# Recommendation model's interaction and MLP, one core: weights split on VectorE, the load order and the first chunk's gram schedule changed

## What is computed

```python
def reference(bottom_output, W0, b0, W1, b1, W2, b2, W3, b3, W4, b4):
    bottom_mlp_output = bottom_output[:, 0, :]
    interaction = jnp.einsum('bnd,bmd->bnm', bottom_output, bottom_output)
    interaction_flat = interaction[:, _TRIL_R, _TRIL_C]      # 351 pairs
    x = jnp.concatenate([bottom_mlp_output, interaction_flat, zero_pad], axis=1)
    x = jax.nn.relu(x @ W0.T + b0)      # 480 -> 1024
    x = jax.nn.relu(x @ W1.T + b1)      # 1024 -> 1024
    x = jax.nn.relu(x @ W2.T + b2)      # 1024 -> 512
    x = jax.nn.relu(x @ W3.T + b3)      # 512 -> 256
    return x @ W4.T + b4                # 256 -> 1
```

## Time and profile before

| | us |
|---|---|
| median of 3 runs | 509.24 |
| lowest and highest | 509.15, 509.42 |
| the profiled execution | 507.79 |
| its span | 506.0 |
| TensorE matmul busy | 478.7 (95%) |
| VectorE busy | 298.9 (59%) |
| ScalarE busy | 241.9 (48%) |
| GpSimd busy | 46.7 (9%) |

### The profile page before, as it was taken

The page is one execution under the profiler, slowest core; times in us unless marked ns, Lnnn a source line. Parts: engine busy times, 40 slices in busy tenths (PEclk is TensorE's granted clock), DMA queues, the critical chain, the costliest instruction groups (busy, mean ns, idle before and its releaser), DMA issues.

```text
span 506.0 us, 6672 instructions
## 1 busy us (share of the span) xinstructions
PE 478.7 (95%) x2480; PEld 401.4 (79%) x2480; DVE 298.9 (59%) x455; ACT 241.9 (48%) x579; POOL 46.7 (9%) x27
## 2 busy tenths in 40 slices
PE   5899678798999999999999999999999999999996
PEld 5899667687888888788888888788888888888874
DVE  3786999658645777858535777858535533110123
ACT  3877376465763347465553347465553411110121
POOL 0446440122230000000000000000000000000000
PEclk9999889899999999999999999999999999999998
DMA  7995055476429131446245242446223100424200
GB/s 259 375 378 191 8 166 196 154 257 241 169 96 345 66 117 61 171 168 227 83 155 189 83 110 66 153 161 229 84 84 110 58 0 1 166 95 155 83 0 2
DMA packets 17456, 72.28 MB, mean 143 GB/s; under 512 B 2448, under 2 KB 2448, under 8 KB 13328
## 3 DMA queue, kind: packets, MB, share of 16 engines
q1 hardware_dynamic: 17424, 71.86, 39.4%
HBM read 63.45 MB, written 8.40 MB: 142 GB/s over the span
## 4 chain that ended last, share of the span: by engine, by line
PE 78%; DVE 11%; issue 5%; ACT 3%; DMA 3%; SPq 0%; ACTq 0%; DVEq 0%
PE work L714 15%; PE work L715 15%; PE work L716 15%; PE gps L739 8%; PE acc L714 7%; PE acc L715 7%; PE acc L716 7%; DMA xraw<-x_t 3%; DVE turned L573 2%; ACT grams L400 1%; PE gps L726 1%; PE acc L726 1%; DVE h1l L612 1%; DVE xpad L633 1%; DVE grams L542 1%
## 5 line engine op out<-in xcount | busy, mean ns | idle before, releaser
L400 ACT ACTIVATE grams<-gps 32x216 f32<-32x216 f32 x384 | 131.5, 343 | 99.5 <-PE gps L739 95.9
L714 PE MATMUL work<-h1h,w1s 128*128 128x512 f32 x256 | 102.4, 400 | 2.0 <-DVE h1l L612 2.0
L715 PE MATMUL work<-h1h,w1s 128*128 128x512 f32 x256 | 102.0, 399 | 0.0
L716 PE MATMUL work<-h1l,w1s 128*128 128x512 f32 x256 | 101.4, 396 | 0.0
L432 ACT ACTIVATE act_out<-work,bias 128x512 f32<-128x512 f32 (+1 forms) x64 | 42.4, 663 | 101.8 <-PE work L716 99.1
L739 PEld LDWEIGHTS gps<-xs 128*128 128x128 f32 x384 | 56.9, 191 | 20.6 <-issue 7.5
L739 PE MATMUL gps<-xs 128*128 128x224 f32 x384 | 59.3, 277 | 9.9 <-DVE featL L601 5.0
L542 DVE SCALAR_TENSOR_TENSOR grams<-grams 128x216 f32<-128x216 f32 x48 | 21.5, 448 | 73.6 <-ACT grams L400 73.6
L714 PE MATMUL work<-featH,w0l 117*128 117x512 f32 (+5 forms) x160 | 58.3, 364 | 3.7 <-ACT act_out L439 3.7
L610 DVE CAST h2h<-act_out 128x512 fp32r<-128x512 f32 x40 | 17.0, 426 | 75.7 <-ACT act_out L432 75.4
L714 PEld LDWEIGHTS work<-h1h,w1s 128*128 128x128 f32 x256 | 48.5, 189 | 12.2 <-DVE h1l L612 2.1
(11 more groups left out here) (68 smaller groups left out, 579.2 us busy)
## 6 DMA issues: line engine op xcount, KB each, us to landing
xraw<-x_t SPq DMA_DIRECT2D x64, 432.0 KB, 4.8
w1s<-w_parts SPq DMA_DIRECT2D x24, 1024.0 KB, 4.8
w_parts<-w1s SPq DMA_DIRECT2D x8, 1024.0 KB, 5.6
stage<-w_t SPq DMA_DIRECT2D x8, 512.0 KB, 6.2
w0raw<-w_t SPq DMA_DIRECT2D x4, 512.0 KB, 7.2
w2raw<-w_t SPq DMA_DIRECT2D x4, 512.0 KB, 6.2
x0raw<-x_t SPq DMA_DIRECT2D x4, 256.0 KB, 5.1
w3raw<-w_t SPq DMA_DIRECT2D x1, 512.0 KB, 7.6
```

The costliest lines, as they stand in the source:

```text
L400: last = act.activation(grams2[rows, h // 2 % 2, at:at + HALF_GROUPS, :, :], src[:, :, :, q * EVEN:q * EVEN + INPUTS], ACT.Copy)
L714: pe.matmul(dst, wl, ah, start=start, stop=False)
L715: pe.matmul(dst, wh, ah, start=False, stop=False)
L716: return pe.matmul(dst, wh, al, start=False, stop=stop)
```

## The change

1. **Low parts of all weights go from GpSimd to VectorE** (`w0_lo_part`, `w1_lo_part`, `w2_lo_part`, `w3_lo_part`, and `zero_pads` for the pads of `xs`). GpSimd keeps only the identity matrix. W0's four are placed in the loop over the first chunk's slices, W1's behind layer 0 and layer 1 tiles, W2's four behind layer 1's tiles 0, 2, 4 and 6, W3's behind tile 7. The single count `w_done` becomes one for each weight.
2. **Input loads first.** Slices 0 to 3 are issued ahead of the small loads (biases, W4, b4); W0's pieces follow slices 4, 6, 7 and 9; slices (1,0) and (1,1), W1 tiles 0 and 1, slices (1,2) and (1,3), then W2 and W3.
3. **TensorE warm-up.** 13 transposes of the identity matrix are put ahead of the first gram.
4. **Two slices earlier.** `input_parts(1, 0)` and `(1, 1)` move into the loop over the first chunk's slices (its passes 13 and 14).
5. **The first chunk's gram schedule.** Halves 0 to 4 stand after steps 6, 11, 16, 21 and 26, then every three steps; a turn stands two steps ahead of its next half instead of three. Halves 4, 8, 12 and 16 are now after steps 26, 38, 52 and 64, half 31 after 113, the last turn after 119. The other chunks keep their schedule.
6. **Conversions.** W1's first two come earlier (within the left half's tiles), W2's four between the early tiles of layer 0, W3's behind W1's tile 3; W1's tiles 2 to 7 keep their places.

```diff
-        for h in range(HALVES):
-            half_at[step] = h
-            sub, behind = divmod(h - TURN_BEHIND, 2 * SLICES_SUB)
-            if behind == 0 and sub >= 0:
-                turn_at[step + APART_STEPS] = sub
-                step += TURN_STEPS
-            else:
-                step += APART_STEPS
-        turn_at[STEPS - 6] = SUBS - 1
+        def plan(starts, gap, last):
+            half_at, turn_at, step = {}, {}, None
+            for h in range(HALVES):
+                step = starts[h] if h < len(starts) else step + 3
+                sub, behind = divmod(h - 1 - TURN_BEHIND, 2 * SLICES_SUB)
+                if behind == 0 and sub >= 0:
+                    turn_at[step] = sub
+                    step += gap
+                half_at[step] = h
+            turn_at[last] = SUBS - 1
...
+        plans = [plan([6, 11, 16, 21, 26], 2, STEPS - 1)] + [plan([1], 3, STEPS - 6)] * (CHUNKS - 2) + [({}, {})]
...
-            load_x(0, 0)
-            sp.dma_start(w4raw[:, :, :], w4).then_inc(small_in, 16)
-            sp.dma_start(bias[:, :], biases).then_inc(small_in, 16)
-            sp.dma_start(bias4[:, :], b4.to_broadcast([P, 1])).then_inc(small_in, 16)
...
+            for p in range(2):
+                load_x(1, p)
+            for m in range(2):
+                load_w1(m)
+            for p in range(2, XSLOTS):
+                load_x(1, p)
+            for n in range(W2_LOADS):
+                sp.dma_start(w2_part(w2raw, n), w2[n, :, :]).then_inc(w2_in[n], 16)
+            sp.dma_start(w3raw[:, :], w3).then_inc(w3_in, 16)
             load_x0(1)
...
-            def w1_lo(m):
-                pool.wait_ge(w_hi, REST + m + 1)
-                pool.tensor_tensor(w1s[:, m % 2, 1, :], stage[:, m % 2, :], w1s[:, m % 2, 0, :].bitcast(f32),
-                                   ALU.subtract).then_inc(w_done, 1)
...
+            def w1_lo_part(m):
+                dve.wait_ge(w1_hi, m + 1)
+                dve.tensor_tensor(w1s[:, m % 2, 1, :], stage[:, m % 2, :], w1s[:, m % 2, 0, :].bitcast(f32),
+                                  ALU.subtract).then_inc(w1_done, 1)
...
+                if LEFT_AT < p < SLICES - 1:
+                    zero_pads(p - LEFT_AT - 1)
+                    input_parts(1, p - LEFT_AT - 1)
+            w1_lo_part(0)
...
+                    if c == 0 and m + 2 < MT1:
+                        w1_lo_part(m + 2)
+                    if c == 0 and m % 2 == 0:
+                        w2_lo_part(m // 2)
+                    if c == 0 and m == MT1 - 1:
+                        w3_lo_part()
...
+            for _ in range(WARM):
+                pe.transpose(acc[:, 3, 0:P], ident[:, :], ident[:, :])
```

More of the change, by code:

```diff
@@ L156, in by_sample, with w2_part @@
             return buf[:, p % XSLOTS, :].rearrange("p (b n) -> p b n", n=INPUTS)
[L158 to L163, removed]
+        def w2_part(buf, n):
+            return buf[:, n * LOAD:(n + 1) * LOAD]
         def parts(g, p):
@@ L196, in rec_program, with before @@
         STEPS = L0_STEPS + L1_STEPS + MT2 * KT2
[L197 removed]
         TURN_BEHIND = 10
[L199 to L211 removed]
+        def plan(starts, gap, last):
[8 more added lines that the diff above has]
+            turn_at[last] = SUBS - 1
+            assert sorted(turn_at.values()) == list(range(SUBS)) and max(half_at) < last < STEPS
+            return half_at, turn_at
+        plans = [plan([6, 11, 16, 21, 26], 2, STEPS - 1)] + [plan([1], 3, STEPS - 6)] * (CHUNKS - 2) + [({}, {})]
+        def before(c, step):
+            half_at, turn_at = plans[c]
             return (sum(x < step for x in half_at), sum(x < step for x in turn_at))
         LEFT, RIGHT = slice(0, CHUNK // 2), slice(CHUNK // 2, CHUNK)
[L218 to L220 removed]
+        SMALL_AFTER = 3
+        W0_AFTER = [4, 6, 7, 9]
+        W0_HI_AFTER = [3, 5, 7, 9]
+        W0_LO_AT = [5, 6, 9, 10]
+        W4_AT = 10
+        WARM = 13
         PAD_AHEAD = 2
@@ L455, in w1_hi @@
                     act.wait_ge(w1_kept[m % 2], kept(m - 2))
[L456 to L461 removed]
+                act.activation(w1s[:, m % 2, 0, :], stage[:, m % 2, :], ACT.Copy).then_inc(w1_hi, 1)
             act.wait_ge(zero_done, 2)
@@ L490, in on_tile @@
                     relu(c, layer, m, work[:, m % 2, :])
-                    if c == 0 and layer == 0 and m < EARLY + 2:
-                        w1_hi(m - EARLY)
+                    if c == 0 and layer == 0 and m == EARLY:
+                        w2_hi_part(2)
+                    if c == 0 and layer == 0 and m == EARLY + 1:
+                        w2_hi_part(3)
                 def after_tile(m):
                     if c == 0 and m + 2 < MT1:
-                        w1_hi(m + 2)
-                interleave(on_half, on_turn, on_tile, after_tile)
+                        w1_hi_part(m + 2)
+                    if c == 0 and m == 1:
+                        w3_hi_part()
+                interleave(c, on_half, on_turn, on_tile, after_tile)
                 for m in range(MT2):
@@ L660, in _ @@
                 split_left(m)
-            for p in range(AHEAD):
-                input_parts(1, p)
+            for i in range(2, XSLOTS):
+                zero_pads(i)
+            input_parts(1, 2)
             def body(c, more):
@@ L677, in on_tile @@
                             answers(c - 1)
+                        if c == 0 and m == EARLY:
+                            w1_lo_part(1)
                     else:
@@ L804, in layer2 @@
                 pe.wait_ge(split_done, nth(c, 1, k) + 1)
+                if c == 0 and k % 2 == 0:
+                    pe.wait_ge(w2_done, k // 2 + 1)
                 for m in range(MT2):
@@ L855, in after_step @@
                     if more and step in half_at:
-                        gram_half(c + 1, half_at[step], before(step)[1])
+                        gram_half(c + 1, half_at[step], before(c, step)[1])
                     if more and step in turn_at:
-                        transpose_pairs(c + 1, turn_at[step], before(step)[0])
+                        transpose_pairs(c + 1, turn_at[step], before(c, step)[0])
                     step += 1
```

118 lines of the change are left out of this document (59 added, 59 removed).

## The result

The changed kernel takes **526.67 us** (median of 4 runs, 525.4 to 527.29) beside 509.25 for the kernel before, run beside it: a ratio of 1.0331, 95% interval 1.0307 to 1.0355. It is slower by 17 us. The forecast was 523.0 with a range of 510 to 533. The profiled execution took 527.29 us, its span is 525.5, against 506.0 before.

A forecast was written before the change was run, and what follows sets the result against it. TensorE was taken to end the kernel. Layer 2 of the first chunk ends at 65.8 + 80.7 + 29 = 175.5; the next chunk starts 13.9 us later; 507.79 + 13.9 = 521.7, plus 1.45 for the median: 523 us, range 510 to 533.

The forecast's parts named there:

- steps 0 to 23 end: Rest of layer 0, right half of the columns, in the first chunk: ends at 65.8 us, 15.2 earlier.
- the four waits: First chunk after step 23: TensorE held up by late W1 loads for 3.4, 7.2, 4.7 and 7.5 us, 22.8 in all.
- half clock behind the four: After each TensorE stop for a late W1 load: matmuls at half clock cost 1.5 us.
- steps, halves, turns otherwise: First chunk after step 23, undisturbed: 96 steps, 28 gram halves and three transposes take 80.7 us.
- waits at the end: Before layer 0 of the second chunk: TensorE waits 3.9 us, 2.1 + 1.8, where it waited for nothing.
- half clock at the end: With the wait before the second chunk's layer 0: half clock costs 1.5 us more.
- the front: Start of the kernel up to the numbered steps: these begin at 53.8 us instead of 60.6.
- The wait that was off most: Second W1-load wait, first chunk: load lands at 29.1 us after step 23, TensorE stands at half 11 for 7.2 us.
- The clock term: Half clock behind TensorE's stops: 1.5 us each, bounded by zero and twice that.
- rival 3: Layer 1 tiles: VectorE becomes the bound, some 2 us more in each of six tiles, 535 us; chance 0.04.
- Rival 1: First chunk: W1 loads still land in time and TensorE runs through, 495.5 us; chance 0.12.
- Rival 2: W1-load waits are shallow: transfers land in 4.3 us and half clock fails to come, 508 us; chance 0.05.

The follow-up runs named there:

- experiment 1: Changed kernel with only SyncE's order rewritten: W1 write-backs and loads ahead of slice loads that wait for later splits; 497.43 us, ratio 0.9776 to the kernel before.
- experiment 2: Changed kernel with only the first chunk's gram schedule put back as in the kernel before; 503.06 us, ratio 0.988 to the kernel before.
- experiment 6: Changed kernel with W1's write-backs and loads of tiles 2 to 7 issued by GpSimd instead of SyncE; 497.84 us, ratio 0.9775 to the kernel before.
- experiment 5: Changed kernel with only W1 tile 0's write-back and tile 2's load moved ahead of slice (1,7) in SyncE's order; 523.64 us, ratio 1.0282.
- experiment 3: Changed kernel with an in-between gram schedule: halves 0 to 4 after steps 4, 8, 12, 16, 20, last turn after 114; 517.72 us, ratio 1.0151.
- experiment 8: experiment 1 plus eight GpSimd subtractions of 1,024 columns into a buffer nobody reads; 513.35 us, ratio 1.0089 to the kernel before.
- experiment 10: experiment 1 with halves 25 to 31 two steps apart, last turn after 117, W3's low part behind tile 5; 498.07 us, ratio 0.9776.

## Why the prediction was right, and where its sizes were off

**Direction and mechanism** are as predicted: weight loads behind slice loads whose splits the new plan puts later, ScalarE in the landing of `stage` four times, for 3.8 to 8.8 us (3 to 9 were foretold), gram copies behind it, TensorE behind those, a fifth stop before layer 0 of the second chunk. Experiments 1, 2 and 6 take the cause away in three ways and the waits go in all three.

**The sum.** Layer 0 of the second chunk starts at 185.2; predicted was 181.0. Term by term:

| | predicted | measured |
|---|---|---|
| steps 0 to 23 end | 65.8 | 66.2 |
| the four waits | 3.4, 7.2, 4.7, 7.5 = 22.8 | 3.8, 9.2, 5.5, 6.8 = 25.2 |
| half clock behind the four | 6.0 | 8.3 |
| steps, halves, turns otherwise | 80.7 | 82.4 |
| waits at the end | 3.9 | 3.1 |
| half clock at the end | 1.5, ahead of layer 0 | 1.4, behind its start |

The measured half clock is the difference of TensorE's busy time in experiment 1 (90.99 less 82.74), the row under it what is left of the 119.0 us; the last row is 342.1 us from layer 0's start to the end against 340.7 before.

The term for the undisturbed steps was 1.7 us short; TensorE's 82.74 us of busy time in experiment 1 show the same. Of that, 0.4 is a slip: with the values as printed, 96 x 0.70, 28 x 0.44 and 3 x 0.25 make 80.3 and not 80.7. Another slip is in the front: 2.1, 3.69 less 0.7 to 1, and 1.5 make 6.3 to 6.6 us and not 6.8.

**The wait that was off most** is the second. I let TensorE run on to half 11. In fact it stopped already at the turn, two steps ahead, because the turn writes to the bank that half 10's copy had not yet left; and the chain from the split of (1,7) to the landing took 8.6 us (88.69 to 97.29) where I had 7.5. **The clock term** was mis-sized too: 1.5 us for each stop came from stretches behind waits of about 3 us. Behind the wait of 9.16 us TensorE worked at half clock from 100.86 to 106.8, and behind that of 5.46 from 121.19 to 127.3; there a matmul of 512 columns starts every 0.43 us instead of every 0.23, so the two cost some 2.7 and 2.8 us.

**Where luck helped.** The profiled execution is 5.6 us over the 521.7 forecast for it, the median only 3.7 over 523: it stands 0.6 us below the profiled execution, where I had added 1.45, and so 2 us of the miss cancelled by chance.

**The front** was right to 0.8 us (steps begin at 54.6, predicted 53.8). VectorE's 1,024-column subtraction, of which the trace before had no row, takes 1.22 us against the 1.2 taken from the slope of rows 7:
```profile
L627 DVE TENSOR_TENSOR w1s<-stage,w1s 128x1024 fp32r<-128x1024 f32 x8 | 9.8, 1223 | 25.9 <-ACT w1s L443 25.9
```
So rival 3, VectorE as the bound, had no price to live on. **Rival 1**, the lead that suffices, would have given 495.5 us; experiments 1 and 6, in which the loads are in time, give 497.4 and 497.8. Its sum was good and its condition false. **Rival 2** (shallow waits) needed landings of 4.3 us and no half clock, and had neither: the shortest of the eight landings is 5.8 us.

**What I had wrong without its showing in the number**: that the four waits add up, and that the lead is a number of steps. Experiment 5 shows the first, experiment 3 the second. The forecast came out because I had walked VectorE's queue row by row for this one plan; counting steps for another plan failed at once.

## What to carry to other kernels

A DMA queue with waits in it is a program of its own: when a schedule is moved on the compute engines, read for every load which unrelated wait stands ahead of it, and where the instruction that ends that wait has gone, in the order of its own engine and not in steps of the busiest one. The repair is a place in the queue, or another queue, and costs nothing: experiment 1 keeps the whole change, adds only the order of SyncE's issues, and is 2.2% faster than the kernel before and 5.4% faster than the changed one. And a stall removed ahead of another is not worth its length: look at which chain ends the next one.

## What the runs showed of the hardware

- A GpSimd subtraction of 1,024 columns (2.46 us) in buffers of its own stopped one VectorE instruction for 2.2 us nearly each time it ran, down to an addition of 13 columns that takes 0.18 us otherwise; eight of them, two of those in the front, made the kernel 15 us longer although nobody waited for them (experiment 8).
- Three of the four stretches of half clock at the long waits outlasted the 3.4 us of the kernel before: about 10, 7 and 7 us, of which 5.9, 6.1 and 3.2 fell on work. Waits of the same length were not treated alike. Behind 1.82 us in front of half 11 the granted clock stayed at 1.00 in experiment 1, and behind 1.83 us at the same place it was 0.50 for some 3 us in experiment 10. One such stretch more or less, 1.5 us, is the size of the differences between the best kernels here.
- Issued by GpSimd, the loads of W1's tiles 2 to 7 landed in 7.7 us (median) and the 1 MB write-backs in 4.6; issued by SyncE in the changed kernel, the loads of all eight tiles landed in 6.7 and the write-backs in 5.7. GpSimd's issues stretched nothing on VectorE.
